# The end of a 48-iteration pipelined kernel written out per engine, with its last batch in token halves

## What is computed

```python
for i in range(DEPTH):                     # DEPTH = 6
    x = attn_layer(shift_tokens(x), Wqkv[i], q_scale[i], k_scale[i], Wo[i]) + x
    x = ffn_layer(shift_tokens(x), ln_g[i], ln_b[i], W1[i], b1[i], W2[i], b2[i]) + x
...
x = _layernorm(x + _L0_ffn_ref(x, ...), axis=-1)

def shift_tokens(t):                       # second half of the features comes from the token before
    a, s = jnp.split(t, 2, -1)
    s = jnp.pad(s, ((0, 0), (1, 0), (0, 0)))[:, :-1]
    return jnp.concatenate([a, s], -1)
```

## Time and profile before

| | us |
|---|---|
| median of 3 runs | 3773.79 |
| lowest, highest | 3773.41, 3777.23 |
| the profiled execution, as timed | 3775.59 |
| its span in the profile | 3773.8 |
| of that, from the end of the loop's last TensorE step to the end | 80.8 |

### The profile page before, as it was taken

The page is one execution under the profiler, slowest core; times in us unless marked ns, Lnnn a source line. Parts: engine busy times, 40 slices in busy tenths (PEclk is TensorE's granted clock), DMA queues, the critical chain, the costliest instruction groups (busy, mean ns, idle before and its releaser), DMA issues.

```text
span 3773.8 us, 133054 instructions
## 1 busy us (share of the span) xinstructions
PE 3586.4 (95%) x47336; PEld 3052.6 (81%) x47336; DVE 3120.3 (83%) x6999; ACT 3373.2 (89%) x10923; POOL 2748.7 (73%) x2058
## 2 busy tenths in 40 slices
PE   7989979999999999999999999999999999999996
PEld 4666668888888888888888888888888888888885
DVE  7888978888888878888788887878888788888984
ACT  7888859989999999999999999899999999999994
POOL 0111159888788888888788888887888888888882
PEclk9999989999999999999999999999999999999998
DMA  2000001111111111111111111111111111111111
GB/s 98 7 11 12 7 23 46 34 33 32 40 46 34 35 31 34 43 41 40 29 36 36 40 46 33 32 31 40 46 35 36 29 35 41 34 34 38 40 37 33
DMA packets 165626, 132.97 MB, mean 35 GB/s; under 512 B 114928, under 2 KB 125552, under 8 KB 164720
## 3 DMA queue, kind: packets, MB, share of 16 engines
q1 hardware_dynamic: 164976, 124.45, 13.4%
HBM read 25.84 MB, written 4.19 MB: 8 GB/s over the span
## 4 chain that ended last, share of the span: by engine, by line
PE 71%; ACT 5%; issue 5%; DVE 5%; ACTq 0%; DVEq 0%; POOLq 0%; POOL 0%
PE bank L926 10%; PE bank L972 9%; PE bank L952 8%; PE bank L1011 8%; PE bank L994 6%; PE bank L891 4%; PE bank L892 4%; PE bank L893 4%; PE bank L865 4%; PE bank L987 3%; ACT a_E L1154 3%; PE bank L849 2%; PE bank L851 2%; PE bank L850 2%; PE bank L905 1%
## 5 line engine op out<-in xcount | busy, mean ns | idle before, releaser
L1208 POOL TENSOR_TENSOR a_rn<-a_ssqc,a_minus_half 128x16 f32<-128x16 f32 x384 | 1113.8, 2901 | 524.6 <-DVE a_ssqc L1379 519.2
L1154 ACT ACTIVATE a_E<-bank,a_negmax 128x96 f32<-128x96 f32 x3072 | 1015.5, 363 | 22.9 <-DVE a_negmax L1328 22.2
L1230 POOL TENSOR_TENSOR a_r<-a_u,a_rn 128x512 f32<-128x512 f32 x768 | 788.7, 1047 | 0.6
L1217 POOL TENSOR_TENSOR a_PN<-a_E,a_erec 128x384 f32<-128x384 f32 x768 | 743.2, 987 | 14.6 <-DVE a_erec L1387 14.5
L1154 ACT ACTIVATION_READ_ACCUMULATOR a_E<-bank,a_negmax 128x1 f32 x3072 | 705.7, 230 | 0.0
L1136 ACT ACTIVATE a_QK<-bank 128x512 f32<-128x512 f32 x768 | 467.1, 608 | 147.1 <-PE bank L926 147.1
L1341 DVE TENSOR_TENSOR a_u<-bank,a_rot_c 128x512 f32<-128x512 f32 x768 | 521.5, 679 | 2.4 <-ACT a_sq L1128 2.4
L1128 ACT ACTIVATE a_sq<-bank 128x512 f32<-128x512 f32 x768 | 483.5, 630 | 44.4 <-PE bank L893 13.7
L1351 DVE TENSOR_TENSOR a_v<-bank,a_rot_s 128x512 f32<-128x512 f32 x768 | 522.2, 680 | 0.0
L1112 ACT ACTIVATE a_PT<-bank 128x512 f32<-128x512 f32 x768 | 486.0, 633 | 25.1 <-PE bank L952 21.6
L926 PE MATMUL bank<-ident,a_r 128*128 128x128 f32 x3072 | 482.9, 280 | 18.1 <-DVE a_bias L1313 11.8
(11 more groups left out here) (140 smaller groups left out, 8412.7 us busy)
## 6 DMA issues: line engine op xcount, KB each, us to landing
a_V_even<-a_V_odd SPq DMA_DIRECT2D x384, 128.0 KB, 2.3
a_V_even<-a_V_odd SPq DMA_DIRECT2D x192, 64.0 KB, 2.1
a_raw<-in_qkv SPq DMA_DIRECT2D x20, 384.0 KB, 3.5
a_x_sh<-X SPq DMA_DIRECT2D x48, 128.0 KB
a_V_even<-a_V_odd SPq DMA_DIRECT2D x192, 32.0 KB, 2.0
a_f_sh<-X SPq DMA_DIRECT2D x48, 128.0 KB
a_x_sh<-X SPq DMA_DIRECT2D x48, 127.0 KB
a_f_sh<-X SPq DMA_DIRECT2D x48, 127.0 KB
```

The costliest lines, as they stand in the source:

```text
L1154: ins = act.activation(E[:, s.par, k, :], p_s[:, i % 2, col:col + KW], ACT.Exp, bias=negmax[:, s.par, k:k + 1], accum_out=esum[:, s.par, k ...
L1208: pool.tensor_tensor(rn[:, a.par, :], ssqc[:, a.par, :], minus_half[:, :], ALU.pow).then_inc(S["rn"], 1)
L1217: pool.tensor_tensor(PN[:, s.par, 2 * hp:2 * hp + 2, :].rearrange("p i (b k) -> p i b k", b=2)[:, :, :, 0:KW], spread(E[:, s.par, half, :] ...
L1230: pool.tensor_tensor(heads(r[:, a.par, half]), heads(u[:, a.par, half]), rn[:, a.par, mm * 2 * HG:(mm + 1) * 2 * HG].unsqueeze(2).to_broad ...
```

## The change

It rewrites what stands behind the 48 iterations; `every_iteration` now ends with n = 47. Each engine has an `end()` with the remaining work listed step by step. Inside the loop only `make_shifter` is new: two memsets and a 128x128 copy on VectorE, once, in the last iteration.

- **Scores in two bank pairs.** Odd pairs of the last four put their scores in banks 0 and 1 (`end_s`), free once the last projection has been read; even ones stay in 3 and 4.
- **VectorE copies probabilities.** From pair -5 (half 1) on, `end_probs` on VectorE takes the copy that ScalarE did.
- **Feed-forward of f = 46 among the drain.** Its transpose goes to bank 4 and its gate and value chunks to banks 3, 4, 3 and 0, 1, 4, between attention outputs. The `down` of f = 45 and of f = 46 use bank 3. Gelu is applied chunk by chunk, and a one-column Gelu behind the last exponentials loads the function's table.
- **Last batch in token halves.** Residual sum, shift, statistics, norm, transpose and split are done for tiles 0 and 1, then 2 and 3. The shift is made by TensorE: three matmuls into bank 0 or 1, one with the identity for the unshifted features and two with `shifter` for the shifted. No DMA takes part. The six chunks of f = 47 have a bank each (2, 4, 7, 5, 6, 0), the `down` of each half its own (3 and 1), and the last norm and the store go by halves.

```diff
+    end_s = lambda s: psum[:, 0:2, 0:4 * KW] if s.k % 2 else p_s
+    end_gates, end_values, end_out = (banks[2], banks[4], banks[7]), (banks[5], banks[6], banks[0]), (banks[3], banks[1])
     def every_iteration(engine, cycle):
-        for n in range(NI + 1):
-            for p in range(NP if n < NI else LAG_Y):
+        for n in range(NI):
+            for p in range(NP):
                 cycle(n, p)
...
-            shift(NI - 1)
+            load_x0(5)
+            store(4)
...
+            def end_shift(half):
+                pe.wait_ge(S["shifter"], 1)
+                pe.wait_ge(S["end_x"], half + 1)
+                pe.wait_ge(S["h"], NF * (NI - 2) + 1 + half)
...
+                pe.matmul(o[:, :, 0:D // 2], ident[:, :], x[:, m, 0:D // 2], start=True, stop=True, skip_group_check=True)
+                pe.matmul(o[:, :, side], shifter[:, 0:P], x[:, m, side], start=False, stop=False, skip_group_check=True)
+                first = 0 if half else 1
+                pe.matmul(o[:, first:2, side], shifter[:, P:2 * P], x[:, 2 * half + first - 1:2 * half + 1, side], start=False, stop=True,
+                          skip_group_check=True).then_inc(S["end_sh"], 1)
...
-            last_feed_forward(NI - 2)
-            last_feed_forward(NI - 1)
+            end()
...
+            def end_probs(j, hp):
+                t = end_pair(j)
+                dve.wait_ge(S[f"pt{hp}"], t.k + 1)
+                dve.wait_ge(S["o"], t.k - 1)
+                dve.tensor_copy(PT[:, t.par, 4 * hp:4 * hp + 4, :], p_t[hp].rearrange("p (n q) -> p n q", n=4)).then_inc(S[f"pt_out{hp}"], 1)
```

More of the change, by code:

```diff
@@ L826, in turn, with up_matmuls, up @@
                     ins.then_inc(S["turned"], 1)
-            def up(n, p, c, part, bank, tail=False):
+            def up_matmuls(l, c, part, bank, x_hi, x_lo):
+                col, rows = up_column(c, part), FCH[c][1]
+                pe.matmul(bank[0:rows, :], w1h[:, l % 2, col], x_hi, start=True, stop=False)
+                pe.matmul(bank[0:rows, :], w1l[:, l % 2, col], x_hi, start=False, stop=False)
+                return pe.matmul(bank[0:rows, :], w1h[:, l % 2, col], x_lo, start=False, stop=True)
+            def up(n, p, c, part, bank):
                 f = n - 2
@@ L846, in up, with down_matmuls @@
                         ge(pe, S["f_out"], f)
[L847 to L851, removed]
+                        ge(pe, S["h"], NF * f + c)
+                    up_matmuls(l, c, part, bank, f_xh[:, :], f_xl[:, :]).then_inc(S["up"], 1)
+            def down_matmuls(l, c, tiles, out, start):
+                rows = FCH[c][1] + (c == NF - 1)
+                for k, i in enumerate(tiles):
+                    ins = pe.matmul(out[:, k * P:(k + 1) * P], h[0:rows, c, i * P:(i + 1) * P], w.w2[0:rows, l % 2, c, :],
+                                    start=(start and k == 0), stop=(c == NF - 1), skip_group_check=True)
+                return ins
             def down(n):
@@ L859, in down @@
                     pe.wait_ge(S["h"], NF * (f + 1))
-                    pe.wait_ge(S["qk_out1"], done(n, P_GELU if n < NI else 0, LAG_T))
-                    ge(pe, S["gate"], NF * (f + 2 if n < NI else f + 1))
+                    pe.wait_ge(S["qk_out1"], done(n, P_GELU, LAG_T))
+                    ge(pe, S["gate"], NF * (f + 2))
                     for c in range(NF):
[L863 to L866, removed]
+                        ins = down_matmuls(l, c, range(MT), p_tb, c == 0)
                     ins.then_inc(S["down"], 1)
@@ L1046, in cycle, with end_queries_and_keys @@
                     down(n)
[L1048 to L1052, removed]
-                        up(n, P_X, c, part, p_t[1 - c % 2], tail=True)
-                down(n + 1)
+            def end_queries_and_keys(j, mm):
+                t = end_pair(j)
+                pe.wait_ge(S[f"r{mm}"], t.k + 1)
+                pe.wait_ge(S[f"pt_out{mm}"], t.k - 4 + mm)
+                qk_transposes(t, mm)
@@ new lines, in end_gate, with end_gelu @@
+            def end_gate(f, c, bank):
+                rows = FCH[c][1]
+                act.wait_ge(S["up"], 2 * NF * f + ((1, 2, 5)[c] if f == NI - 2 else c + 1))
+                act.wait_ge(S["h"], NF * (f - 1) + c + 1)
+                act.activation(gate[0:rows, c, :], bank[0:rows, :], ACT.Identity,
+                               bias=bias[0:rows, f // NB % 2, 2 * c:2 * c + 1]).then_inc(S["gate"], 1)
+            def end_gelu(f, c):
+                act.wait_ge(S["gate"], NF * f + c + 1)
+                act.activation(gate[:, c, :], gate[:, c, :], ACT.Gelu).then_inc(S["end_gelu"], 1)
```

528 lines of the change are left out of this document (411 added, 117 removed).

## The result

The changed kernel takes 3746.17 us in the median (3741.97 to 3746.96, 4 runs), the kernel before 3773.93 beside it, so the two medians differ by 28 us. The ratio of the two is estimated at 0.9922 (interval 0.9905 to 0.994), which is 29 us. The forecast was 22.1 us, and its range began at 3746, where the measured ratio makes 3744 of the 3773.79 us shown before. The profiled execution has a span of 3745.1 us, 28.7 shorter than before.

A forecast was written before the change was run, and what follows sets the result against it. The end was taken as bound by waits, one engine handing to the next. Its stages 38.35 + 6.5 + 7.45 + 3.9 + 2.5 sum to 58.7 instead of 80.85 us, 22.1 less: median 3751.7, range 3746 to 3761.

The forecast's parts named there:

- Nothing of the loop is rewritten ... So only the end can move: Loop: instruction lists agree but for three small VectorE instructions, so its time was held fixed, last row starting at 3692.5.
- A: Drain, from the last row's first four transposes to the last output projection: 38.35 us instead of 41.1; bounds 35.9 and 45.8.
- The clock in A: Rival: the clock falls once in the new end, adding 5.0 us for 3756.7; chance 16%.
- The handovers are not saved: Rival in the drain: it keeps 41.1 us plus 4.6 of moved-in work, 45.7, total 3759.1; chance 11%.
- VectorE's copy: Drain: VectorE's copy of probabilities taken at 0.65 us, bounds 0.50 to 0.70.
- The two bank pairs remove the waits: Drain: scores in two bank pairs let all four exponential groups follow each other by 3713, removing the waits.
- Table load: ScalarE's table load moves to 3713: 1.28 us by the trace's row; the skill's page adds about 1.38 of drain.
- B: Last batch made ready for its feed-forward, to the end of the low part: 6.5 us instead of 20.1; bounds 5.5 and 9.5.
- C: Last batch's feed-forward, to the end of `down`: 7.45 us instead of 11.9; bounds 7.0 and 9.5.
- D: Last norm, half 0 summed after 10 of 12 `down` matmuls: 3.9 us instead of 5.3.
- E: Store at the very end: stays 2.5 us, one half's store following the other.
- What would show it: Signs in the end: exponentials done by 3713, last projection ending at 3731, last `down` at 3745, PEclk 1.00 up to 3742.

The follow-up runs named there:

- the kernel with `exp1` last: Changed kernel with TensorE's wait for the last exponentials' release of the score banks put back behind the two `qk_out` waits in the loop: ratio 0.995, 3754.9 us.
- the one with the four late waits first: Changed kernel with four more TensorE waits of the loop reordered so that the one that comes last is written first: ratio 0.9881, span 3731.8 us.
- `exp1` first: Kernel before with TensorE's wait for the exponentials' release of the score banks written ahead of the two `qk_out` waits: ratio 0.9974.
- the semaphores' numbers: Kernel before with only the changed kernel's 15 semaphores added to its list, so that the others get its numbers: ratio 1.0004.
- the trace with the moved statistics: Changed kernel with VectorE's last-norm statistics of batch 5 moved behind the copies TensorE waits for, its norm further back too: ratio 0.9921.
- the three kernels with all late waits first: Changed kernel with four loop waits reordered (0.9881); plus moved statistics and two more wait orders (0.9865); plus `make_shifter` moved out of the loop (0.987).

## Why the prediction was right or wrong, point by point

- **"Nothing of the loop is rewritten ... So only the end can move"** is the step that failed. The lists of instructions do agree, but the order of three waits ahead of the scores does not, and it was in the whole diff. It is worth 0.37 us in the median iteration, 16.6 us over the 45 between first and last copy; of these 9.5 show, since the longer iterations near a layer change gain only 0.1 to 0.3 us and three of them lose 1.3 each to a clock that had not fallen there before (last section). The first copy starts 0.4 us later and `make_shifter` takes another 0.4 net, which leaves the 8.8 us. The row that pointed there was in the profile of before: idle time of the scores' loads given to "issue", 51.6 us, though a release had just come. The prediction's own last sentence named the sign, the start of the last row at 3692.5; it was 3683.68. With this step out, in the kernel with `exp1` last, the time is 3754.9, just above the range that the prediction gave 50% (3749.5 to 3754.5).
- **A** was mis-sized by 2.75 us. TensorE's waits came as walked, 4.7 us against 4.85, but the one behind VectorE's statistics was 1.99 us and not 1.4. The statistics block took 2.63 us (3707.74 to 3710.37) and not 2.2; the rows that the 2.2 was read from give 2.33 (3766.74 to 3769.07). Its variance took 0.67 us, where the same instruction takes 0.17 at 3734.37; in three traces with the block at this place (this one, the kernel with `exp1` last, the one with the four late waits first) it takes 0.67 to 0.68 and ends 0.02 to 0.04 us behind GpSimd's scaling of two groups of probabilities. No run took the two apart, so that GpSimd's work holds it up is not shown.
- **The clock in A**: it fell once, 1.5 us behind the end of that wait, for 3.4 us. The same end in the kernel with `exp1` last kept the clock and has an A of 39.4, so the fall cost 1.7 us of the 2.75, not the rival's 5.0. By the Trainium skill ("TensorE: Matmul & The Clock Gate", Part 1) idleness takes the full clock back; the trace agrees in that the fall came behind the longest wait, but a wait of 2.0 us stands at this place in five traces, and the clock fell behind it in two of them. Most of the rest of the 2.75 are chunks that stand alone between other work: 0.76 to 1.03 us from start to next start where 0.70 was taken (3723.42 to 3724.18, 3720.62 to 3721.65), 0.8 us over the four at full clock. Some 0.3 us stays unassigned.
- **"The handovers are not saved"**: A would have been 45.7 us; it was 41.1. The moved-in 4.6 us of work fitted into A's old length. VectorE took over ten copies, not eleven.
- **VectorE's copy** 0.65 us: 1.27 for two. **Shift** 0.69 (3722.73 to 3723.42) for 0.7. **Two-column power** 0.70 for 0.69.
- **The two bank pairs remove the waits**: shown, some 4 us. **VectorE's copies**: with them or without them the drain at full clock takes 39.4 us.
- **Table load**: ScalarE's exponentials end at 3704.33, the load takes the same 1.28 us as the row of before, and the next activation follows it at once:

```profile
3704.09 0.24 ACT L1343 ACTIVATION_READ_ACCUMULATOR a_E<-bank,a_negmax 128x1 f32 x1
3704.35 1.28 ACT L1416 ACT_TABLE_LOAD   x1
3705.65 0.20 ACT L1416 ACTIVATE a_first_exp<-a_minus_half 128x1 f32<-128x1 f32 x1
```

  Only 0.02 us lie between the exponentials and the load and 0.02 between the load and the next activation, so the row was the right choice. The 1.38 us of drain of the Trainium skill ("ScalarE: Activation LUTs", What ACT_TABLE_LOAD costs) do not show here.
- **B, C, D, E**: 19.9 us against 19.4 of gain forecast for B to E together. In B the reason is shown, the DMAs. In two traces of the loop's experiments (`exp1` first, and the semaphores' numbers) the end is as in the kernel before, but the clock did not fall in B, which then takes 18.2 us: 1.9 of the 20.1 were the clock's. So part of the 19.9 us is that fall in the one trace of before, and no work saved. C's and D's halves and order were not tried apart.
- **make_shifter**: 0 taken, at most 0.4. Moved out of the loop it gives back 0.6 us; that it is the copy of 0.70 us with VectorE's maxima behind it fits the rows and was not tried apart.
- **What would show it**: statistics of half 0 0.05 us behind the shift, no DMA between sum and norm, last exponentials 20.2 us after the loop's cut (20.0), a wait over 1 us behind the statistics: all seen. The last projection and the last `down` came 2.75 and 2.7 us later behind the loop's cut than said, as A did. PEclk 1.00 up to 3742: not, 0.72 in 3712 to 3718.

## What to carry to other kernels

Compare not only the instructions of a loop but the order of the waits in front of each: write the one that comes last first. Idle time that the profile gives to "issue" in front of a weight load, right behind the release of what it needs, is the sign; five such sites made the loop 28 us shorter (first to last copy 2999.7 to 2971.5 us), some 3 of them because the clock no longer fell at two layer changes. In a drain, keep long blocks of other work off the engine that feeds TensorE: behind one block of 2.6 us TensorE waited 2.0 us, and in two of five traces the clock then fell, for 1.7 more.

## What the runs showed of the hardware

- From a release to TensorE's weight load it was 52 ns with the late wait written first, 69 with it in the middle of three, 113 with it last. The first matmul moved by up to 90 ns.
- The granted clock fell to 0.50 (1.2 GHz) behind idle stretches of TensorE, in some executions and not in others at the same place. At a layer change of the changed kernel's loop, below, TensorE is busy 1.03 of 3 us and then at half clock for most of the next 3 us, and the iteration takes 70.7 us. At 1839 us of the same loop it takes 70.7 where the clock falls and 69.1 in the trace with the moved statistics, where it does not: a fall cost 1.6 us. Falls came at five layer changes in the changed kernel's trace, at two in that of before, and at none in the three kernels with all late waits first; whether the orders of the waits keep it away was not tried:

```profile
1303.00:1306.00 3.00, 1.03 (x10) 1.06 (x11) 3.00 (x7) 1.21 (x7) 2.15 (x3) 1.00 0.00 0
1306.00:1309.00 3.00, 3.00 (x15) 2.61 (x14) 1.21 (x6) 2.19 (x10) 3.00 (x2) 0.53 0.28 63
```

- Before the loop the same falls come at places that differ from run to run. The same stretch of the kernel before, and of the kernel with only other semaphore numbers:

```profile
259.00:263.00 4.00, 4.00 (x29) 2.54 (x27) 3.82 (x19) 3.60 (x12) 0.53 (x1) 1.00 0.00 0
```
```profile
259.00:263.00 4.00, 4.00 (x18) 2.97 (x16) 3.25 (x15) 3.21 (x11) 2.04 (x2) 0.57 0.00 2
```

  The first `a_f_xh` copy started anywhere from 644.7 to 656.1 us in the thirteen traces: by 647.6 in the six with nine falls ahead of it, behind 652 in the six with eleven to thirteen. For a change of a few us the stages of the trace tell more than the times do.
